# The feed-forward stage of a vision-transformer kernel: y turned by a DMA instead of TensorE, its conversion given to VectorE, one of two output tiles to ScalarE and GpSimd

## What is computed

```
z = layernorm(h)
up, gate = split(bitlinear(z, w_in, g_in))        # 192 -> 2 x 512
y = silu(gate) * up
out = h + bitlinear(y, w_out, g_out)              # 512 -> 192

bitlinear(x, w, g):  xn = x * rsqrt(mean(x*x) + 1e-6) * g
                     s = 127 / max(abs(xn));  xq = round(xn * s) / s
                     wq = ternary(w) / scale;  return xq @ wq
```

## Time and profile before

| what | value |
|---|---|
| profiled execution, its own time | 1195.78 us |
| its span, first to last instruction | 1194.0 us |
| median of the three timed runs | 1194.58 us |
| mean granted TensorE clock | 0.988 of full speed |
| busy share PE / DVE / ACT / POOL | 93% / 88% / 77% / 39% |
| feed-forward in its steady part | 930 to about 1187 us |

### The profile page before, as it was taken

One profiled execution on the slowest core, in us unless ns is written; L12 is line 12 of the kernel. 1 busy time (PEld: TensorE's weight loads), 2 busy tenths in 40 slices (PEclk: granted clock), 3 DMA queues, 4 the chain that ended last, 5 costly groups with the idle time before them and its releaser, 6 DMA issues.

```text
span 1194.0 us, 32030 instructions
## 1 busy us (share of the span) xinstructions
PE 1108.2 (93%) x11210; PEld 674.9 (57%) x11210; DVE 1056.6 (88%) x2028; ACT 923.6 (77%) x1832; POOL 466.1 (39%) x498
## 2 busy tenths in 40 slices
PE   7999999889999999999999999999867888888887
PEld 6999998445555555555555555555534444444444
DVE  7687666599999999999999999999887999999996
ACT  0000001889999999999999999999637999999997
POOL 5644344302211223221111232221236777766774
PEclk9999999999999999999999999999879999999999
DMA  8998998445655566556555655555532333333332
GB/s 292 313 314 249 316 306 236 137 138 150 152 150 150 131 147 156 145 150 150 145 150 147 141 150 151 149 151 143 146 98 64 105 101 101 103 99 99 99 95 71
DMA packets 157284, 187.87 MB, mean 157 GB/s; under 512 B 42864, under 2 KB 118464, under 8 KB 156928
## 3 DMA queue, kind: packets, MB, share of 16 engines
q1 hardware_dynamic: 115680, 156.92, 42.2%
q0 software_dynamic: 15936, 10.88, 9.4%
q10 hardware_dynamic: 25536, 18.31, 4.8%
HBM read 143.11 MB, written 36.12 MB: 150 GB/s over the span
## 4 chain that ended last, share of the span: by engine, by line
PE 73%; ACT 10%; issue 7%; DMA 3%; DVE 3%; POOL 2%; SPq 1%; ACTq 1%; DVEq 0%; POOLq 0%
PE psum L1139 14%; PE psum L1197 12%; PE psum L1260 12%; PE psum L1230 7%; PE psum L1200 7%; PE psum L1213 6%; PE psum L1247 6%; PE psum L1326 5%; ACT yi L674 3%; ACT zi L682 2%; ACT big L667 2%; PE psum L1306 1%; PE psum L1316 1%; DMA big<-xt 1%; POOL big L797 1%
## 5 line engine op out<-in xcount | busy, mean ns | idle before, releaser
L1075 DVE TENSOR_TENSOR pi<-big 128x2364 int16<-128x2364 f32 (+1 forms) x128 | 333.8, 2608 | 13.5 <-DMA big<-z_row 13.0
L769 POOL DMA_DIRECT2D h_res<-att x128 | 146.8, 1301 | 492.7 <-ACT att L601 484.0
L625 ACT ACTIVATE big<-psum 128x788 f32<-128x788 f32 (+1 forms) x384 | 330.3, 862 | 5.1 <-PE psum L1247 2.8
L587 ACT ACTIVATE qki<-psum 128x394 int16<-128x394 f32 x384 | 172.4, 508 | 25.5 <-PE psum L1200 13.8
L1139 PE MATMUL psum<-big 128*128 128x192 f32 (+1 forms) x1128 | 185.0, 327 | 2.3 <-DMA big<-xt 2.0
L1139 PEld LDWEIGHTS psum<-big 128*128 128x128 f32 (+1 forms) x1128 | 180.3, 188 | 5.5 <-DMA big<-xt 2.6
L1260 PE MATMUL psum<-big,sa_hot 128*32 128x197 f32 (+1 forms) x3072 | 168.2, 336 | 0.6 <-DVE zt L1099 0.6
L587 ACT ACT_TABLE_LOAD x1 | 1.3, 1283 | 189.5 <-PE psum L1200 189.5
L797 POOL TENSOR_TENSOR big<-big,goutb 128x512 f32<-128x512 f32 (+1 forms) x99 | 123.8, 1270 | 59.5 <-DVE big L1042 59.4
L1247 PE MATMUL psum<-qkb 64*128 64x197 bf16 (+1 forms) x1536 | 128.9, 246 | 1.3 <-DVE qkb L860 1.3
L596 ACT ACTIVATE vi<-psum 128x384 int16<-128x384 f32 (+1 forms) x256 | 115.7, 529 | 4.0 <-PE psum L1200 3.7
(11 more groups left out here) (109 smaller groups left out, 1812.6 us busy)
## 6 DMA issues: line engine op xcount, KB each, us to landing
big<-z_row SPq DMA_DIRECT2D x192, 394.0 KB, 5.0
big<-xt SPq DMA_DIRECT2D x98, 384.0 KB, 4.7
tin<-h_res SPq DMA_DIRECT2D x49, 192.0 KB, 3.0
tres<-h_res SPq DMA_DIRECT2D x49, 192.0 KB, 2.5
out<-oo SPq DMA_DIRECT2D x49, 192.0 KB, 2.6
h_res<-big ACTq DMA_DIRECT2D x84, 96.0 KB, 4.5
h_res<-att POOLq DMA_DIRECT2D x64, 96.0 KB, 3.4
x_int<-big ACTq DMA_DIRECT2D x84, 64.0 KB, 4.4
```

What stands on the lines that cost most here:

```text
L587: act.activation(qki[:, k, :, :], psum[:, bank, 0:2 * N] .rearrange("p (c n) -> p c n", c=2), ACT.Copy, scale=factor[(F_Q, F_K)[b % 2]])\
L625: act.activation(ex[0:r, tri, t, 4 * g:4 * g + 4, :].rearrange("p (a h) n -> p a h n", a=2), psum[0:r, 2 * t:2 * t + 2, 0:2 * N] .rearrang ...
L769: pool.dma_start(h_res[bass.ds(b - 4, 1), t0:t0 + r, :].rearrange("a n d -> (a n) d"), att[0:r, par, t, :], accum_op=ALU.add).then_inc(s_a ...
L1075: v.tensor_tensor(pi[0:r, t, :, 0:N], ex[0:r, it, t, :, :], zb[0:r, ip, :, :], ALU.mult).then_inc(s_pi, 1)
```

## The change

- SyncE turns y: a transposing DMA from `yi3` in SBUF (128 rows of 1024 numbers of 2 bytes, 256 KB) into `yTi`, 8 blocks of 128x128 in the old buffer `qki`, one a step (lag 4, last in SyncE's order). It waits for the scaled y of the same step. SyncE's order is now: load of `tin`, wait for output counts, `tres` (lag 5), store (lag 7), turn.
- TensorE's 8 transposes of y are gone. The second matmuls move from lag 5 to lag 6 and write two PSUM banks, one for each output tile. `keep_busy` is 12 matmuls instead of 8.
- VectorE converts the turned y from int16 to bf16 (128x1024 elements, lag 6), placed between the maximum of y and the first factor operation. It makes only the first of the two output tiles (lag 6).
- ScalarE's joint activation of 1536 columns becomes one of 96x512 for z alone. At the end of its step it scales the second output tile from PSUM into `osc` (128x192, lag 6).
- GpSimd adds the residual to it (128x192, lag 7), between its second power (789) and the products (797), behind three waits.
- `LAGS` is 8 instead of 7, so the pipeline has one more step.

```diff
-        LAGS = 7
+        LAGS = 8
@@ SyncE, pair_step
-                if pair(4) or pair(6):
-                    wait_apart(sp, s_t["o_ready"], min(t - 5, NPAIR) if isinstance(t, int) else t - 5)
-                if at := pair(4):
-                    r, n = at
-                    sp.dma_start(tres[0:r, par, 0:n, :], pair_rows(h_att, t - 4, r, n)).then_inc(s_t3b[par], 16)
-                if at := pair(6):
-                    r, n = at
-                    sp.dma_start(pair_rows(out, t - 6, r, n), oo[0:r, par, 0:n, :]).then_inc(s_t3o[par], 16)
                 if at := pair(-1):
 ...
                     wait_apart(sp, s_t["zc"], t)
                     sp.dma_start(tin[0:r, oth, 0:n, :], pair_rows(h_att, t + 1, r, n)).then_inc(s_t3[oth], 16)
+                if pair(5) or pair(7):
+                    wait_apart(sp, s_t["o_ready"], min(t - 6, NPAIR) if isinstance(t, int) else t - 6)
+                    wait_apart(sp, s_t["o_added"], min(t - 6, NPAIR - 1) if isinstance(t, int) else t - 6)
+                if at := pair(5):
+                    r, n = at
+                    sp.dma_start(tres[0:r, oth, 0:n, :], pair_rows(h_att, t - 5, r, n)).then_inc(s_t3b[oth], 16)
+                if at := pair(7):
+                    r, n = at
+                    sp.dma_start(pair_rows(out, t - 7, r, n), oo[0:r, oth, 0:n, :]).then_inc(s_t3o[oth], 16)
+                if at := pair(4):
+                    r, n = at
+                    wait_apart(sp, s_t["yi"], t - 3)
+                    wait_apart(sp, s_t["yT_read"], t - 5)
+                    sp.dma_start_transpose(yTi[:, par, 0:4 * n, 0:r], yi3[0:r, par, 0:n, :].rearrange("p a h -> p (a h)"))\
+                      .then_inc(s_ym[par], 16)
@@ ScalarE, pair_step
-                if pair(2) == pair(5) == (128, 2):
+                if at := pair(2):
+                    r, n = at
                     act.wait_ge(s_t["xT_summed"], t - 1)
-                    act.wait_ge(s_t["yT_summed"], t - 4)
-                    act.activation(zyT[:, par, :], turned.bitcast(i16)[:, 512:2048], ACT.Copy)\
+                    act.activation(zT3[:, par, 0:n, :, 0:r], psum[0:KH, 4, :].bitcast(i16)[:, 0:512]
+                                   .rearrange("p (a c n) -> p a c n", a=2, c=2)[:, 0:n, :, 0:r], ACT.Copy)\
                        .then_inc(s_t["xT_read"], 1)
 ...
                     act.wait_ge(s_t["factors"], t)
-                    wait(act, s_t["yT_summed"], t - 5)
+                    if not isinstance(t, int) or t > 5:
+                        act.wait_ge(s_ym[par], loads_of(t - 6, par))
 ...
+                if (at := pair(6)) and at[1] == 2:
+                    act.wait_ge(s_t["o_summed"], t - 5)
+                    act.wait_ge(s_t["dequant"], t - 2)
+                    wait(act, s_t["o_added"], t - 7)
+                    act.activation(osc[:, par, :], psum[:, 5, 0:D], ACT.Copy, scale=ft[:, (q + 2) % 4, 1, 1:2])\
+                       .then_inc(s_t["o_scaled"], 1)
@@ GpSimd, pair_step, between lines 790 and 791
+                if (at := pair(7)) and at[1] == 2:
+                    wait_apart(pool, s_t["o_scaled"], t - 6)
+                    wait_apart(pool, s_t3b[oth], loads_of(t - 7, oth))
+                    if not isinstance(t, int) or t > 8:
+                        wait_apart(pool, s_t3o[oth], loads_of(t - 9, oth))
+                    g.tensor_tensor(oo[:, oth, 1, :], osc[:, oth, :], tres[:, oth, 1, :], ALU.add)\
+                        .then_inc(s_t["o_added"], 1)
@@ VectorE, pair_step, ahead of factors(0)
+                if at := pair(6):
+                    r, n = at
+                    dve.wait_ge(s_ym[par], loads_of(t - 6, par))
+                    wait(dve, s_t["o_summed"], t - 6)
+                    v.tensor_copy(yT3[:, 0:n, :, 0:r].rearrange("p a c n -> p (a c) n"), yTi[:, par, 0:4 * n, 0:r])\
+                     .then_inc(s_t["yT_read"], 1)
@@ VectorE, last in its step (lag 5, both tiles, before)
+                    v.scalar_tensor_tensor(oo[0:r, par, 0, :], psum[0:r, 6, 0:D], ft[0:r, (q + 2) % 4, 1, 0:1],
+                                           tres[0:r, par, 0, :], ALU.mult, ALU.add).then_inc(s_t["o_ready"], 1)
@@ TensorE, pair_step
-                if at := pair(5):
-                    r, n = at
-                    pe.wait_ge(s_t["yi"], t - 4)
-                    y_turned(t - 1)
-                    dst = psum[:, 5, :].bitcast(bf16).rearrange("p (a c n) -> p a c n", a=2, c=4)
 ...
-                if at := pair(5):
-                    r, n = at
-                    y_turned(t)
-                    wait(pe, s_t["o_ready"], t - 5)
+                if at := pair(6):
+                    r, n = at
+                    pe.wait_ge(s_t["yT_read"], t - 5)
+                    wait(pe, s_t["o_ready"], t - 6)
+                    wait(pe, s_t["o_scaled"], t - 6)
                     for a in range(n):
                         for c in range(4):
-                            last = mm(psum[0:r, 6, a * D:(a + 1) * D], yT3[:, par, a, c, 0:r], woutb[:, c, :],
+                            last = mm(psum[0:r, 6 - a, 0:D], yT3[:, a, c, 0:r], woutb[:, c, :],
                                       start=(c == 0), stop=(c == 3))
 ...
-                    keep_busy(7, 8)
+                    keep_busy(7, 12)
```

More of the change, by code:

```diff
@@ L183, in vit_tower_kernel @@
             "xT_summed", "xT_read", "hid", "silu", "y", "square", "yg", "y_amax", "y_rms",
-            "yi", "yT_summed", "yT_read", "o_summed", "o_ready")}
+            "yi", "yT_read", "o_summed", "o_ready", "o_scaled", "o_added")}
         s_t3 = [sem(f"ffn_in_{p}") for p in range(2)]
         s_t3b = [sem(f"ffn_residual_{p}") for p in range(2)]
+        s_ym = [sem(f"ffn_y_turned_{p}") for p in range(2)]
         s_sq0 = sem("ffn_first_square")
@@ L339, in vit_tower_kernel @@
         zi3 = sb("zi3", [128, 2, 2, D], i16)
+        yTi = qki[:, :, :, :].rearrange("p a b n -> p (a b n)")[:, 0:2048].rearrange("p (i k n) -> p i k n", i=2, k=8)
+        zT3 = sb("zT3", [KH, 2, 2, 2, 128], bf16)
         xflat = xring[:, :, :].rearrange("p a b -> p (a b)")
@@ L1043, in pair_step @@
                                                silu[0:rr, a, :], ALU.mult, ALU.mult).then_inc(s_t["y"], 1)
[L1044 removed]
+                if at := pair(6):
                     r, n = at
[L1046 to L1055 removed]
+                    dve.wait_ge(s_t["o_summed"], t - 5)
+                    dve.wait_ge(s_t["dequant"], t - 2)
+                    dve.wait_ge(s_t3b[par], loads_of(t - 6, par))
+                    if not isinstance(t, int) or t > 7:
+                        dve.wait_ge(s_t3o[par], loads_of(t - 8, par))
+                    v.scalar_tensor_tensor(oo[0:r, par, 0, :], psum[0:r, 6, 0:D], ft[0:r, (q + 2) % 4, 1, 0:1],
+                                           tres[0:r, par, 0, :], ALU.mult, ALU.add).then_inc(s_t["o_ready"], 1)
             def image_step(b, par, tri):
@@ L1308, in pair_step @@
                     last.then_inc(s_t["xT_summed"], 1)
-                if at := pair(5):
-                    r, n = at
-                    pe.wait_ge(s_t["yi"], t - 4)
-                    y_turned(t - 1)
-                    dst = psum[:, 5, :].bitcast(bf16).rearrange("p (a c n) -> p a c n", a=2, c=4)
-                    for a in range(n):
-                        for c in range(4):
-                            last = nc.tensor.transpose(dst[:, a, c, 0:r], yi3[0:r, oth, a, c * 128:(c + 1) * 128].bitcast(bf16),
-                                                       ident[0:r, 0:r])
-                    last.then_inc(s_t["yT_summed"], 1)
                 if at := pair(3):
```

37 lines of the change are left out of this document (5 added, 32 removed).

## The result

| | before | after |
|---|---|---|
| median of four runs each, us | 1194.46 (1193.99 to 1195.80) | 1219.83 (1218.72 to 1222.58) |
| ratio, 95% interval | | 1.021 (1.020 to 1.023) |
| span of the profiled execution, us | 1194.0 | 1218.6 |
| last pair: start of its scaling of z, us | 1174.94 | 1193.48 |
| from there to the end, us | 19.05 | 25.07 |

The changed kernel is 25 us slower, where 4.5 were forecast, and lies outside the range. The trace splits the 24.5 us of span in two: 18.5 are there when the last pair's z is scaled, and 6.0 come after it. Of the 18.5, the first seven pairs of the feed-forward give 1.3 us back; the 42 steps behind them lose 19.8, that is 0.47 each, and 0.53 in the middle.

The account below looks back on a forecast made before the run. The prediction saw two bounds within 0.05 us: ScalarE's own work (5.83 us) and the circle of the scales (mean 5.81). Terms -2.2 + 4.2 + 2.5 = +4.5 us on 1194.58 gave 1199.1 us, range 1189 to 1213.

Parts of the forecast that it names:

- circle of the scales: ScalarE's scaling of y through squares, GpSimd's power and VectorE's factors back to ScalarE: 5.91 us long, 5.70 short, mean 5.81.
- gain of 0.05 a step: ScalarE: freeing it brings the step from 5.86 to 5.81 and no further, -2.2 us over 44 steps.
- one step in four: GpSimd's addition holds up the last factor operation in 11 steps at 0.38 us each, +4.2 us.
- comes too late to hurt: GpSimd's addition in short steps: factor 986 starts at T + 1.77, line 789 ends at T + 1.80, so no collision.
- T: Start of GpSimd's power of y (line 780) in a step, the zero point for times within it.
- 0.1 us either way decides: Argument for the rival that the step mix stays and the addition never collides: 1194.9 us, chance 0.24.
- collision everywhere: Rival: GpSimd's addition holds up VectorE's factors in every step, +16.7 us, 1211.6 us in all; chance 0.12.
- VectorE's conversion: Ahead of VectorE's factors: 0.47 us fits into 0.60 of cover, price 0, at most 0.26 a step.
- short form: Step form with 986 ending at T + 1.93, circle 5.70; rival with it in every step: 1190.1 us, chance 0.19.
- The turn, SyncE and TensorE: DMA turn hidden (issue 3.0, landing 4.3 us), `tin` fits by 0.2, TensorE's added matmuls off the path: price 0.
- The end: From last scaled y to last output operation: 1.37 us becomes about 3.9, +2.5 us, ends 1.5 and 6.
- 0.26 x 44: Rival that the conversion does not fit beside GpSimd's powers: 0.26 a step, 11 us, about 1209; chance 0.05.

Follow-up runs that it names:

- e3: Kernel before plus a spare GpSimd addition of 128x192 numbers behind its second power: 1208.19 us, ratio 1.012.
- e8: Kernel before plus a spare VectorE conversion of 128x1024 numbers, int16 to bf16, ahead of the first factor operation: 1203.01 us, ratio 1.006.
- e9: Kernel before plus SyncE's turn of the scaled y by DMA into a spare buffer, last in its step: 1198.15 us, ratio 1.002.
- e5: Changed kernel with 8 instead of 12 unread matmuls: 1221.48 us, ratio 1.022 to the kernel before.
- e2: Changed kernel with the output split taken back, VectorE making both tiles, no ScalarE scaling or GpSimd addition: 1205.31 us, ratio 1.010 to the kernel before.
- e12: Changed kernel, conversion behind the last factor, addition waiting for it, 8 unread matmuls ahead of the second matmuls and 2 behind: 1207.57 us, ratio 1.010.
- e1: Changed kernel with GpSimd's addition also waiting for the same step's factors: 1205.47 us, ratio 1.009 to the kernel before.
- e4: Kernel before plus a GpSimd memset of about the addition's length behind its second power, writing only: 1195.66 us, ratio 1.001.
- e13: e12 with the conversion between the two products of y and the addition waiting for the factors instead: 1215.73 us, ratio 1.016 to the kernel before.

## Why the prediction was wrong

**The bound, right.** ScalarE is idle ahead of line 671 in all 39 steps, released by the last factor. The circle of the scales decides, and the earlier trace rows had it with its two forms. The gain of 0.05 a step was at most 0.02: ScalarE starts 0.08 behind the last factor on the mean, and 0.10 before.

**ScalarE, right.** 0.40 for the scaling of 192 columns (0.4 forecast), 0.58 for z's activation (0.67 forecast). The work that went was hidden from the path, as the prediction said.

**GpSimd's addition, the step that failed.** Mechanism and size were right: 0.31 to 0.45 forecast for a collision; the last factor lasts 0.45 more in after (0.61 against 0.16) and ends 0.41 later in e3. The charge of "one step in four" was wrong: it is every step. Two small assumptions carried that charge. The prediction put the addition 0.08 us behind the end of line 789 and concluded that in the short steps it "comes too late to hurt". In e3 and in after it starts 0.03 before the power's recorded end, between T + 1.77 and T + 2.24 in the steps of after, each time in the very instant in which the last factor starts. And it took a tie to go VectorE's way; in after both start at 1052.72 and VectorE waits. From 930 us on 40 of them are 0.60 long or more: in place of +4.2 stand 0.45 x 40 = 18 us.

That the two meet is no accident of the timing. The trace of before has it already: in 22 of the 31 steps between 960 and 1140 us the second power is longer than 0.71, and in each of these it ends 0.03 us behind the start of line 986, as in the earlier trace rows (1056.33 and 1056.30); in the other 9 it ends 0.23 ahead of it, as in the earlier trace rows. In all 28 steps of after it is of the first kind. An instruction behind such a power that starts 0.03 before its end starts with the last factor, wherever in the step that is; behind the other kind it starts ahead of line 988 and stops that one (e3, 0.46). Both ways collide. So the prediction's "0.1 us either way decides", and its chance of 0.12 for the collision everywhere, treated as loose what the trace shows tied.

**VectorE's conversion, wrong by a small term.** Its length was right (0.42, 0.47 forecast), its price of 0 was not. The first factor starts at T + 0.93 instead of T + 0.81. The mean hides two things: in 6 of 28 steps the conversion starts with the power and makes it 0.30 longer, and the short form, in which the first factor starts 0.03 behind the power, is found in one step of four and no longer in two; in the others it is 0.20 behind. In e8, where VectorE has no room, the price is 0.23 a step. The prediction's upper end was 0.26. It took 0 because the second power lasted 0.70 beside line 997 in one step; in others of the same trace it lasts up to 0.93.

**The sum of a step.** Before 5.86; the first factor starts 0.11 later, from there to the end of the last factor it takes 0.44 more, and ScalarE follows 0.02 sooner: 6.39, as measured. The loss over all 42 steps is 0.47 each, since the first and last ones, written out, lose less.

**The turn, SyncE and TensorE, right.** Issue 1.25 us (between 1.2 and 3.0; 3.0 taken), landing 3.2 (4.3 taken), hidden. `tin` landed in time, with more room than the 0.2 us forecast, since the issue was shorter. e9 bounds what the turn costs in the steps by 0.07 each, 3.7 us of span, and those lie in a wait on ScalarE. Twelve matmuls for eight are free (e5). The figure that the prediction quotes from the Trainium skill (VectorE: DVE Perf Modes, section "The three transpose paths") is for one block of 128x128; eight in a row, an estimate of 10.5 us, do not describe this turn, which took 3.2.

**The end, the wrong path.** +2.5 forecast with ends 1.5 and 6; it measured 6.0, the upper end. The terms of the sum (issue, landing, conversion, matmuls) lead from the last scaled y to the last output operation. They were nearly right: 4.28 us after, 1.37 before, 2.9 more. But the last output operation does not end the kernel. GpSimd's DRAIN does; before, it is over 2.0 us behind the one of SyncE, so 2.0 of those 2.9 us would have been hidden, and e2, which has the turn and not the split, is 1.3 longer at its end. The other 4.8 are GpSimd's addition: it is now GpSimd's last instruction and starts 6.0 us later than the last one did. The prediction left the split out of the end altogether; that its upper end of 6 was met is luck.

**Together.** Of the 19.8 us that the 42 steps lose, the forecast had 2.0. By the means of the middle the addition (0.44 a step, less the 4.2) is short by 14.3, the conversion (0.11) by 4.6, and the gain of ScalarE that did not come by 1.4; the written-out steps, which lose less, take back about 2.5. The end is short by 3.5, and the first pairs gave 1.3 back: 4.5 + 14.3 + 4.6 + 1.4 - 2.5 + 3.5 - 1.3 = 24.5, as measured; the 2.5 is what closes the sum. Of the rivals the one with the collision in every step named the mechanism, at 1211.6; its 8 missing us are the conversion and the end. Two of the round figures for rivals do not come out of their terms to the us: 0.26 x 44 on top of the forecast is 1210.5, not 1209, and 17.6 on top of it 1216.7, not 1215. Nothing hangs on them.

**Left open.** Why VectorE's short form turns up in one step of four rather than two was read from the trace, and no run takes it apart. Nor does one say why the second power lasts up to 0.93 in some steps and 0.69 in others; that its longer forms end 0.03 behind the start of VectorE's last factor suggests that VectorE's operations hold it up, and is not shown. Nothing tried beats the kernel before. e12, e1 and e2 come to within 10 to 13 us of it, and in all three the conversion or what depends on it is in the way of a step that had no slack to give.

## What to carry to other kernels

Before an instruction with SBUF inputs is given to GpSimd, look at what VectorE reads in the same half microsecond: an addition of 0.59 us, which fits into GpSimd's idle time, cost 0.38 us a step in e3, because VectorE's operation of 0.16 us was on the critical circle. When two such instructions abut to within 0.1 us, price the collision in every step. A wait that lets the short critical one go first gave more than half of the loss back (e1).

Work that leaves a full engine is worth only what its own circle leaves it, here at most 0.05 us of a step; read the circle first, then the busy share. And an item that seems to lag by a whole step may be needed next in its own engine's order: follow it once around before it is moved.

At the end of a kernel, look for the engine that finishes last with everything behind it. Here GpSimd's closing DRAIN of 8.3 us sets the end, so a late last instruction on GpSimd is paid for in full, while VectorE's and SyncE's last work had 2 us to spare in the kernel before.

## What the runs showed of the hardware

- A waiting GpSimd instruction gets in between two VectorE operations that follow each other without a gap: the addition started at 1052.72, as 998 ended and 996 began, and 996 took 0.61 us.
- A conversion on VectorE of 128x1024 from int16 to bf16 (0.42 us) holds up a GpSimd power over 2 numbers a row in both orders. Where it starts up to 0.02 behind the power, or ahead of it, the power ends 0.56 us behind the conversion (1.00 long in after; 0.85 and 0.89 in e5). Where it is still running at T + 0.71 or later, the power ends 0.03 to 0.04 behind it (0.75 to 1.01 long in e1, e2 and e8). In between, started at T + 0.03 to T + 0.20 and over by T + 0.62, it leaves the power its 0.70.
- Where GpSimd's second power was longer than 0.71 us, it ended 0.03 us behind the start of VectorE's last factor operation: 22 of 31 steps before, all 28 of after, 21 of 29 in e3. In e13 it was over 0.3 to 0.4 us ahead of that start.
- A GpSimd memset of 0.59 us in the same place holds up nothing (e4, 5.86 us a step as before).
- A turn by DMA of 128x1024 numbers of 2 bytes from SBUF to SBUF took 1.25 us to issue and 3.2 to land, for eight blocks of 128x128, while the stage moved 134 GB/s.
- With 8 unread matmuls a step of 6.38 us the granted clock was 0.95 of full speed, with 12 it was 1.00; the time was the same within the intervals.
- GpSimd's DRAIN at the end of the kernel took 8.27 to 8.31 us in every one of the 14 kernels and started with GpSimd's last instruction; in 13 of them, all but e2, the span ended some 0.2 us behind it.
